# Weights split ahead of the last heads, a square that reads the bank, and a query product between score tiles

## The reference

```python
x = x + tanh(g_xattn[0]) * L0_xattn(layernorm(x), ctx)   # 32 heads of 128, 8 kv heads, q and k RMS-normalised
x = x + tanh(g_ffn[0])   * L0_ffn(layernorm(x))          # relu(h @ up)**2 @ down, plus a routed part; layernorm
x = x + tanh(g_xattn[1]) * L1_xattn(layernorm(x), ctx)   # 32 heads of 16, 8 kv heads
x = x + tanh(g_ffn[1])   * L1_ffn(layernorm(x))          # quantised to 8 bits, silu gate
```

## Time and profile before

| | |
|---|---|
| timed runs, median of 3 (lowest to highest) | 1005.25 us (1004.34 to 1007.79) |
| the profiled execution's own time | 1001.03 us |
| its span in the trace | 999.1 us |
| mean granted TensorE clock over the span | 0.989 |
| PE busy, PEld busy | 955.8 us (96%), 828.9 us (83%) |
| DVE busy | 643.4 us (64%) |
| ACT busy | 479.3 us (48%) |
| POOL busy | 356.0 us (36%) |

### The profile page before, as it was taken

The page is one execution under the profiler, slowest core; times in us unless marked ns, Lnnn a source line. Parts: engine busy times, 40 slices in busy tenths (PEclk is TensorE's granted clock), DMA queues, the critical chain, the costliest instruction groups (busy, mean ns, idle before and its releaser), DMA issues. The chain is left out here.

```text
span 999.1 us, 18524 instructions
## 1 busy us (share of the span) xinstructions
PE 955.8 (96%) x6876; PEld 828.9 (83%) x6876; DVE 643.4 (64%) x1102; ACT 479.3 (48%) x937; POOL 356.0 (36%) x244
## 2 busy tenths in 40 slices
PE   4989999999999999999999999999989998999996
PEld 3879989998998899899989989898967777777755
DVE  5567557656755774675577467556734875788856
ACT  4356336534643653464356346535614512566644
POOL 3335317243541633344154324423134620170033
PEclk9989999999999999999999999999999998899999
DMA  6020203201210220032021102100134304843001
GB/s 231 1 65 32 55 1 84 63 0 22 73 53 0 84 52 11 0 94 53 0 74 29 44 0 84 63 0 11 22 91 164 114 13 149 200 59 64 2 1 43
DMA packets 40677, 55.01 MB, mean 55 GB/s; under 512 B 8640, under 2 KB 20544, under 8 KB 40640
## 3 DMA queue, kind: packets, MB, share of 16 engines
q1 hardware_dynamic: 40064, 54.49, 20.0%
q10 hardware_dynamic: 576, 0.00, 0.0%
HBM read 50.22 MB, written 4.26 MB: 55 GB/s over the span
## 5 line engine op out<-in xcount | busy, mean ns | idle before, releaser
L440 DVE TENSOR_TENSOR ptL<-tbank,ptH 128x512 fp32r<-128x512 f32 x192 | 132.2, 689 | 69.4 <-ACT ptH L309 66.9
L309 ACT ACTIVATE ptH<-tbank 128x512 fp32r<-128x512 f32 x192 | 115.5, 601 | 110.9 <-PE tbank L556 110.5
L556 PE MATMUL tbank<-ident,probs 128*128 128x128 f32 x864 | 132.7, 276 | 6.7 <-DVE ptL L440 3.4
L453 DVE TENSOR_REDUCE negmax<-score 128x1 f32<-128x768 f32 x128 | 120.4, 950 | 10.8 <-PE score L80 10.3
L330 ACT ACTIVATE probs<-score,negmax 128x768 f32<-128x768 f32 x128 | 115.5, 903 | 18.3 <-DVE negmax L453 18.3
L78 PE MATMUL obank<-ptH,vH 128*128 128x256 f32 x384 | 121.4, 316 | 0.0
L411 DVE TENSOR_REDUCE sumsq<-probs 128x2 f32<-128x256 f32 (+1 forms) x80 | 42.0, 526 | 115.4 <-ACT probs L304 71.8
L556 PEld LDWEIGHTS tbank<-ident,probs 128*128 128x128 f32 x864 | 97.9, 140 | 17.5 <-DVE ptL L440 10.2
L217 POOL TENSOR_TENSOR rnorm<-sumsq,neg_half 128x2 f32<-128x2 f32 (+1 forms) x80 | 71.4, 895 | 107.8 <-DVE sumsq L413 107.7
L80 PE MATMUL obank<-ptH,vL 128*128 128x256 f32 x384 | 108.8, 283 | 0.0
L80 PE MATMUL score<-wkvH,kvT_lo 128*128 128x256 f32 x384 | 108.7, 283 | 0.0
(11 more groups left out here) (263 smaller groups left out, 2249.6 us busy)
## 6 DMA issues: line engine op xcount, KB each, us to landing
wqo_stage<-in_wq SPq DMA_DIRECT2D x9, 1024.0 KB, 5.4
wqo_stage<-in_wo SPq DMA_DIRECT2D x8, 1024.0 KB, 7.2
factors<-r_scratch SPq DMA_DIRECT2D x32, 256.0 KB, 4.0
wkv_stage<-in_wkv SPq DMA_DIRECT2D x9, 512.0 KB, 6.2
a_qS<-q_scratch SPq DMA_DIRECT2D x24, 128.0 KB, 5.3
ctx_stage<-in_ctxT SPq DMA_DIRECT2D x2, 1024.0 KB, 13.2
kS<-k_scratch SPq DMA_DIRECT2D x32, 64.0 KB, 3.5
q_scratch<-qpart SPq DMA_DIRECT2D x16, 128.0 KB, 1.9
```

What stands on the lines that cost most here:

```text
L309: act.activation(out, tbank[c % 2][:], ACT.Copy, scale=scale).then_inc(t_hi, 1)
L440: i = dve.tensor_tensor(out, tbank[c % 2][:], f32(hi), ALU.subtract)
L453: dve.tensor_reduce(negmax[:, m:m + 1], score[m % 2][:, 0:SKV], AX.X, ALU.max, negate=True).then_inc(s_max, 1)
L556: i = pe.transpose(tbank[c % 2][:, n * P:(n + 1) * P], block_in, S.ident[:])
```

## The change

Five edits around the two borders of the first feed-forward:

1. In `last()` of the first attention SP issues the load of `wkv1` ahead of the four factor spreads, and POOL splits these weights ahead of all four `o_lo_part`s instead of between head 1 and head 2.
2. The square of an up tile reads its first operand from the PSUM bank (bank times relu) instead of from SBUF. The bank is thereby in use until the square is done: `up_tile(j)` and the fc2 step wait for `h_done` instead of `relu_done`, and the wait for `relu_done` ahead of the down product is gone.
3. POOL makes each weight's low part in two halves of its columns.
4. `qpart` has room for both batches, and ACT no longer waits for the stores of batch 0.
5. The last query product (b = 1, m = 3) moves from the end of the feed-forward to between `scores(0, 0)` and `scores(0, 1)`; the DVE step that belongs to it moves between the maxima of the two.

```diff
@@ attn0, sync, last()
                 S.load_wo(sp, LAST)
+                sp.wait_ge(wkv_split, NS * LAST + NS)
+                sp.dma_start(S.wkv_stage[:], A.wkv1.rearrange("(t p) n -> p t n", p=P)).then_inc(S.wkv1_in, 16)
                 for h in range(GRP):
                     spread_factors(LAST, h)
-
-                sp.wait_ge(wkv_split, NS * LAST + NS)
-                sp.dma_start(S.wkv_stage[:], A.wkv1.rearrange("(t p) n -> p t n", p=P)).then_inc(S.wkv1_in, 16)
@@ attn0, gpsimd, last()
                 split_wo(LAST)
-                o_lo_part(LAST, 0)
-                o_lo_part(LAST, 1)
                 pool.wait_ge(pe_kv, NKV * LAST + NKV)
                 split(wkvH[:], wkvL[:], S.wkv_stage[:], S.wkv1_in, 0, S.wkv1_split)
-                for h in range(2, GRP):
+                for h in range(GRP):
                     o_lo_part(LAST, h)
@@ ffn0
-        xnT1, qpart = lsb("xnT1", [P, KT, ROWS], fp32), lsb("qpart", [P, NQ, 2, SQ], f32r)
+        xnT1, qpart = lsb("xnT1", [P, KT, ROWS], fp32), lsb("qpart", [P, B, NQ, 2, SQ], f32r)
...
+    def halves(w):
+
+        n = w.shape[2] // 2
+        return [(slice(None), slice(None), slice(i * n, (i + 1) * n)) for i in range(2)]
...
+    def last_project(pe):
+
+        pe.wait_ge(*free_q[B - 1][NQ - 1])
+        project_query(pe, B - 1, NQ - 1)
+    S.last_project, S.last_low = last_project, lambda dve: query_low(dve, B - 1, NQ - 1)
@@ ffn0, gpsimd
             pool.wait_ge(w_hi, c + 1)
-            pool.tensor_tensor(lo, staged(c), f32(hi), ALU.subtract).then_inc(w_split, 1)
+            for cols in halves(hi):
+                i = pool.tensor_tensor(lo[cols], staged(c)[cols], f32(hi)[cols], ALU.subtract)
+            i.then_inc(w_split, 1)
@@ ffn0, vector
-            dve.tensor_tensor(relu[:, i % RT, :], relu[:, i % RT, :], relu[:, i % RT, :], ALU.mult).then_inc(h_done, 1)
+            dve.tensor_tensor(relu[:, i % RT, :], bank[4 + i % 2][:], relu[:, i % RT, :], ALU.mult).then_inc(h_done, 1)
@@ ffn0, scalar
-                if b:
-                    act.wait_ge(S.q_out[m], 32)
@@ ffn0, tensor
             if j >= 2:
-                pe.wait_ge(relu_done, j - 1)
+                pe.wait_ge(h_done, j - 1)
...
         pe.wait_ge(exp_lo, NL)
-        pe.wait_ge(relu_done, NI)
...
                 pe.wait_ge(w_split, ready["fc2"])
+                pe.wait_ge(h_done, NI)
...
-            for m in range(NQ):
+            for m in range(NQ - b):
@@ attn1, vector
-        for t in range(2):
-            maxima(0, t)
+        maxima(0, 0)
+        S.last_low(dve)
+        maxima(0, 1)
@@ attn1, tensor
-        for t in range(2):
-            scores(0, t)
+        scores(0, 0)
+        S.last_project(pe)
+        scores(0, 1)
```

More of the change, by code:

```diff
@@ L770, in ffn0, with project_query, query_low @@
     tr1_bank = [bank[0], bank[1], bank[6], bank[7]]
+    def project_query(pe, b, m):
+        for k in range(KT):
+            i = pe.matmul(qbank[b][m][:, 0:SQ], S.wqo_stage[:, k, m * P:(m + 1) * P],
+                          xnT1[:, k, b * SQ:(b + 1) * SQ], start=k == 0, stop=k == KT - 1)
+        i.then_inc(pe_q, 1)
+    def query_low(dve, b, m):
+        dve.wait_ge(q_hi, NQ * b + m + 1)
+        dve.scalar_tensor_tensor(qpart[:, b, m, 1, :], qbank[b][m][:, 0:SQ], float(D1) ** -0.5,
+                                 f32(qpart[:, b, m, 0, :]), ALU.mult, ALU.subtract).then_inc(q_lo, 1)
+    def last_project(pe):
+        pe.wait_ge(*free_q[B - 1][NQ - 1])
+        project_query(pe, B - 1, NQ - 1)
+    S.last_project, S.last_low = last_project, lambda dve: query_low(dve, B - 1, NQ - 1)
+    free_q = [[(y_copied, 3), (y_done, 1), (y_done, 2), (y_copied, 4)], [(xnT1_done, 1), (xnT1_done, 2), (q_lo, 1), (q_lo, 2)]]
     def sync(sp):
@@ L799, in sync @@
                 for r in range(2):
-                    sp.dma_start(S.q_dram[r, m * P:(m + 1) * P, cols], f32(qpart[:, m, r, :])).then_inc(S.q_out[m], 16)
+                    sp.dma_start(S.q_dram[r, m * P:(m + 1) * P, cols], f32(qpart[:, b, m, r, :])).then_inc(S.q_out[m], 16)
                 if m == 1:
@@ L893, in vector @@
         normalise_1(RT - 1)
-        for b in range(B):
-            for m in range(NQ):
-                dve.wait_ge(q_hi, NQ * b + m + 1)
-                dve.scalar_tensor_tensor(qpart[:, m, 1, :], qbank[b][m][:, 0:SQ], float(D1) ** -0.5,
-                                         f32(qpart[:, m, 0, :]), ALU.mult, ALU.subtract).then_inc(q_lo, 1)
+        for n in range(B * NQ - 1):
+            query_low(dve, n // NQ, n % NQ)
     def scalar(act):
@@ L972, in scalar @@
                 act.wait_ge(pe_q, NQ * b + m + 1)
-                if b:
-                    act.wait_ge(S.q_out[m], 32)
-                act.activation(qpart[:, m, 0, :], qbank[b][m][:, 0:SQ], ACT.Copy,
+                act.activation(qpart[:, b, m, 0, :], qbank[b][m][:, 0:SQ], ACT.Copy,
                                scale=float(D1) ** -0.5).then_inc(q_hi, 1)
@@ L1063, in tensor @@
             i.then_inc(pe_fc2, 1)
-        free_q = [[(y_copied, 3), (y_done, 1), (y_done, 2), (y_copied, 4)], [(xnT1_done, 1), (xnT1_done, 2), (q_lo, 1), (q_lo, 2)]]
         for b in range(B):
@@ L1074, in tensor @@
             pe.wait_ge(xnT1_done, 2 * b + 2)
-            for m in range(NQ):
+            for m in range(NQ - b):
                 pe.wait_ge(*free_q[b][m])
[L1077 to L1080, removed]
+                project_query(pe, b, m)
     return Programs(sync, gpsimd, scalar, vector, tensor)
```

## The result

| | before | after |
|---|---|---|
| timed runs, median (lowest to highest) | 1004.8 us (1003.61 to 1007.79), 4 runs | 990.07 us (989.88 to 991.59), 4 runs |
| ratio after to before | | 0.9869, 95% interval 0.9838 to 0.99 |
| the profiled execution's own time | 1001.03 us | 990.12 us |
| its span | 999.1 us | 988.3 us |
| mean granted TensorE clock over the span | 0.989 | 0.998 |

The kernel is 1.3% faster: 14.7 us between the medians, 10.9 us between the two profiled executions.

What follows compares the result with a forecast made beforehand. PE, busy for 96% of the span, was taken as the bound, so only its idle gaps counted. Gains of 3.9 + 2.3 + 0.3 = 6.5 us, taken from a median of 1005.25, gave 998.7 us; range 992.5 to 1003.0.

Steps and rivals of the forecast that it cites:

- New stall: Start of the second attention: PE waits 0.8 us for the query loads, a wait the fourth query product had covered.
- The path terms: Gains at the first attention's end, up stage and second attention's start: 3.9 + 2.3 + 0.3 = 6.5 us.
- the low end of the range: Whole-kernel time of 992.5 us: the half-clock case with 2 us for the scatter of timed runs.
- the half clock goes too: Second attention's start: the moved dense product also removes the 1.2 GHz stretch, 4.1 us more, giving 994.6 us; chance 0.27.
- the first gap: End of the first attention: PE idles 3.44 us ahead of head 2, at full clock, counted against the clock case.
- The timed median lies 4.2 us above it: Whole kernel: timed median 1005.25 against 1001.03 us profiled, unexplained; the same saving was taken from the median.
- the clock rival: Second attention's start: dense work removes the low-clock stretch, saving 4.1 us beyond the forecast; chance 0.27.

Runs made afterwards that it cites:

- d3: The changed kernel with the square read from SBUF again and the waits on `relu_done` back, POOL's halves kept: 993.75 us, ratio 0.9904.
- d2: The changed kernel with POOL making each weight's low part in one whole piece again: 990.81 us, ratio 0.9888.
- b0: The kernel before, unchanged, run once more to see the spread of its times and clocks: 1003.85 us, ratio 0.9996.
- b3: The kernel before with an unread equal of one query product (eight matmul records) between the first two pairs of score tiles: 998.98 us, ratio 0.9941.
- d1: The changed kernel with the last query product back in its old place and two unread fp32 products between the score tiles: 990.22 us, ratio 0.9868.
- b2: The kernel before with 14 unread 512-column matmuls where PE waits for head 2 of the output projection: 1002.19 us, ratio 0.9965.
- c4: The changed kernel with the last query product back ahead of the first score tile, room for both batches kept: 994.22 us, ratio 0.9905.
- c1: The changed kernel with the `wkv1` load and split back in their old places: 996.33 us, ratio 0.9945.
- c2: The kernel before with only the square from the PSUM bank and POOL's low parts in halves: 1000.85 us, ratio 0.997.
- c3: The kernel before with only the room for both batches' queries and the last query product between the score tiles: 998.32 us, ratio 0.9957.

## Why the prediction was wrong in its time, though its stalls were right

**Edit 1: right.** Predicted: the split at 691.1 to 695.5, low part 2 from 724.6 to 725.9, PE at head 2 at 732.35, head 3 ready 2.3 us ahead of PE, 3.9 us gained. Measured: 691.09 to 695.44, 724.76 to 726.06, 732.27, low part 3 done at 732.82 and head 3 begun at 735.07 (2.25 us), 4.06 us gained.

**Edits 2 and 3: the sum right, the share of edit 3 wrong.** The squares are 0.69 us beside POOL (predicted 0.68) with one operand in a bank, as against 0.68 with none where POOL is quiet. The Trainium skill, VectorE: DVE Perf Modes, section on the TRN2 errata, gives 120 fixed cycles from PSUM against 58 from SBUF; the 0.5 us that this made for eight squares is not in the rows. The low parts are at most 1.76 us outside the last merged pair (predicted at most 1.9). The first down matmul follows the last up matmul directly, and the gain to the batch 0 queries is 6.32 - 4.06 = 2.26 us (predicted 2.3). But I gave the halves a part in it, by the page SBUF — State Buffer of the Trainium skill, section on the two sides of SBUF. The alternation that it describes is in the rows of d3. Halving POOL's instruction did cut DVE's longest steps where both have two operands in SBUF (1.78 us in d3, 1.91 to 2.90 in the earlier trace rows), but the stage took no less time for it, 79.58 us against 79.52; and with the square on the bank whole instructions were as good or better (d2). The 2.3 us are edit 2's alone.

**Edits 4 and 5: right in the stalls.** New stall 0.92 us (predicted 0.8), the four maxima done at 834.77 + 1.28 = 836.05 (predicted 842.2, less the 6.3 us of before: 835.9), gain to unit 0's exponential 6.61 - 6.32 = 0.29 us (predicted 0.3).

The path terms are then 6.6 us against a forecast of 6.5, and the lowest times say much the same: before never took less than 996.75 us in 82 runs, the change took 989.88 at best, 6.9 us less.

**Where it failed: from the sum to the time.** Two steps of the prediction did this, and with them the low end of the range came out too high.

*The clock as a rival at 0.27.* The case "the half clock goes too" is what happened, with 4.4 us against the 4.1 that I worked out. I held the first gap against it: the longest gap, 3.44 us, had cost no clock. That was one execution read as a rule. b0 shows the same gap with a fall behind it (0.66 from 735 to 740 us), and the same second border without one; of six traces with that gap mine was the only one without the fall. The rows had what was needed: the clock fell behind thin, 64-row tiles with gaps between, and the change put dense work just there. b3 and d1 show that this is enough.

*"The timed median lies 4.2 us above it, and I have no row for that."* I carried the saving of the path to that median as if the 4.2 us were fixed. They aren't. The times of this program go with the mean granted clock (over the three sets, 0.994 or more at 996.75 to 998.88 us, 0.984 or less at a median of 1006.4), so most executions have more clock falls than the profiled one. One of these falls is located: the one behind the first gap, 1.1 to 2.3 us. The timed runs ahead of the prediction have no clock on record; one more set of runs with it, as in b0, would have told. Taking away the gaps takes away the falls behind them. From the profiled execution the clock rival would have been 1001.03 - 6.5 - 4.1 = 990.4, and 990.12 was measured. The low end of 992.5 left it out because it started from 1005.25.

The account of the 14.7 us: 6.6 on the path; 4.4 for the fall at the second border (b3: 4.35 by filling alone); 1.1 to 2.3 for the fall behind the first gap (1.1 in b2 and in four traces, 2.3 in b3's). These are 12.1 to 13.3. The 1.4 to 2.6 us left stay open, and may be nothing: the interval of the ratio allows a gain of 10.0 to 16.3 us. Only profiled executions have a clock by stretch, so where an unprofiled run of 1004 us or more lost its clock isn't shown; in c4 one further fall stands at 877 to 882 us (0.66), behind the second border. Some scatter isn't the clock: from unit 3's exponential to the end of the span the 13 traces without a fall there take 141.3 to 142.8 us.

## What to carry to other kernels

Read the mean granted clock of every timed run beside its time before a saving is carried to the median: where the two go together, the gaps that the change closes also pay in clock, and the sum starts from the run whose clock is known. A thin stretch with small gaps can cost more than it idles (4.4 us behind a gap of 1.4), and the full-width matmuls put into it here, useful or not, got that back. When GpSimd and VectorE meet on SBUF, move one operand to PSUM first; cutting GpSimd's instruction in halves was no substitute: without the move PE still stood 1.8 us (d3), and the halves brought nothing, with it (d2) or without it (79.58 us for the stage in d3, 79.52 before).

## What was not expected of the hardware

- The clock did not follow the program alone: the same kernel's second border ran at 1.00 in b0 and at 0.50 in the earlier trace rows, and its runs lie between 996.75 and 1010.04 us. Why it falls in one execution and not in the next isn't shown.
- A gap of 3.5 us cost little when the clock fell behind it (b2: 1.1 us by filling it; 1.1 us in the traces of b0, c1, c2 and c3, 2.3 in b3's), a gap of 1.4 us behind thin tiles 4.4 us (b3: 4.35 by filling it). In b0's rows the matmuls were back at 0.39 us at 738.88 us, 3.3 us after the first of 0.63, with matmuls of 512 columns at work; at the second border, with 64-row and 128-column matmuls at work, it was back only after unit 3, some 14 us later.
- Taking turns costs both engines: in d3 two halves of POOL take 3.45 us instead of the 2.56 of a whole one, and each of DVE's steps 1.78 instead of 0.68. With one operand in PSUM the DVE step kept its 0.69 us.
